# Decoder layer on one core: hand-written steps of a slot replaced by a finer table of ticks

## The reference

```
x = x + attention(layernorm(x))          # 16 heads of 8, causal, rope, keys and values through a latent of 32 with its own norm
x = x + cross_attention(layernorm(x))    # 8 heads of 64, 32 context rows per batch
x = x + ffn(layernorm(x))                # gate/up/down with 352 hidden; inputs and weights rounded to blocks of 16 FP4 values
```

## Time and profile before

| | us |
|---|---|
| median of 3 runs | 427.41 (425.40 to 429.64) |
| the profiled execution: span from first to last instruction | 431.1 |
| busy: PE, DVE, ACT, POOL | 295.3, 301.2, 177.1, 194.2 |

### The profile page before, as it was taken

The page is one execution under the profiler, slowest core; times in us unless marked ns, Lnnn a source line. Parts: engine busy times, 40 slices in busy tenths (PEclk is TensorE's granted clock), DMA queues, the critical chain, the costliest instruction groups (busy, mean ns, idle before and its releaser), DMA issues.

```text
span 431.1 us, 6518 instructions
## 1 busy us (share of the span) xinstructions
PE 295.3 (69%) x1790; PEld 144.0 (33%) x1790; DVE 301.2 (70%) x1137; ACT 177.1 (41%) x327; POOL 194.2 (45%) x374
## 2 busy tenths in 40 slices
PE   1702655777888788787868687787878846657454
PEld 1300233332343222324333334344343314436233
DVE  5426749472666546878886898989978356787872
ACT  5320345563544454443555454454446313222111
POOL 4200216761133534545384745535447353745653
PEclk9999999996766655886997798989969869766696
DMA  6079000043030025002100260030000000000000
GB/s 186 0 207 209 1 0 2 2 149 74 1 75 1 0 76 147 2 2 59 23 8 0 81 149 6 3 79 3 9 6 2 8 0 8 6 1 7 2 13 18
DMA packets 20835, 17.50 MB, mean 41 GB/s; under 512 B 1920, under 2 KB 20224, under 8 KB 20800
## 3 DMA queue, kind: packets, MB, share of 16 engines
q1 hardware_dynamic: 20272, 16.50, 15.7%
q10 hardware_dynamic: 528, 0.59, 0.5%
HBM read 9.62 MB, written 7.34 MB: 39 GB/s over the span
## 4 chain that ended last, share of the span: by engine, by line
PE 36%; DVE 30%; issue 10%; POOL 9%; DMA 7%; ACT 5%; SPq 1%; POOLq 0%; DVEq 0%; ACTq 0%
DVE summed L832 7%; PE pvp L1116 7%; PE st L1105 4%; PE mxp L1081 4%; DMA ks<-parts_dram 3%; PE mxp L1016 3%; DVE space L766 2%; PE misc L1180 2%; DMA parts_dram<-parts 2%; POOL space L473 2%; DVE space L763 2%; PE misc L1195 2%; PE pvp L1127 2%; DVE space L746 2%; ACT probs L633 2%
## 5 line engine op out<-in xcount | busy, mean ns | idle before, releaser
L832 DVE CUSTOM_DVE_ANT_0 summed<-mxp,causal 128x512 bf16<-128x512 f32 (+3 forms) x256 | 114.0, 485 | 28.2 <-PE mxp L1081 27.9
L633 ACT ACTIVATE probs<-st 128x1024 f32<-128x1024 f32 (+1 forms) x96 | 84.6, 881 | 85.4 <-PE st L1105 85.1
L1081 PE MATMUL mxp<-ks,qs 48*128 48x512 bf16 (+3 forms) x256 | 41.4, 362 | 62.2 <-DVE rmax L832 38.6
L443 POOL TENSOR_SCALAR_AFFINE_SELECT probs<-probs 128x256 f32<-128x256 f32 x128 | 49.6, 423 | 24.8 <-ACT probs L633 24.8
L1116 PE MATMUL pvp<-probs,va 128*32 128x128 f32 (+3 forms) x512 | 57.1, 530 | 5.1 <-POOL probs L443 5.1
L543 ACT ACTIVATE space<-misc 128x128 f32<-128x128 f32 (+3 forms) x78 | 24.2, 327 | 50.9 <-PE misc L1136 18.0
L1105 PE MATMUL st<-qs,ks 50*128 50x512 bf16 (+3 forms) x256 | 41.7, 366 | 4.6 <-ACT probs L633 2.5
L1081 PEld LDWEIGHTS mxp<-ks,qs 48*128 48x128 bf16 x256 | 11.9, 98 | 82.6 <-DVE rmax L832 44.6
L473 POOL TENSOR_TENSOR space<-space 128x128 f32<-128x128 f32 (+2 forms) x33 | 24.8, 751 | 19.7 <-DVE space L769 19.7
L434 POOL TENSOR_SCALAR var<-mv 128x1 f32<-128x1 f32 (+1 forms) x36 | 9.1, 253 | 46.1 <-DVE mv L739 44.6
L485 POOL TENSOR_TENSOR space<-space,reciph 128x352 f32<-128x352 f32 x16 | 12.6, 786 | 35.1 <-DVE reciph L757 35.1
(11 more groups left out here) (196 smaller groups left out, 587.9 us busy)
## 6 DMA issues: line engine op xcount, KB each, us to landing
parts_dram<-parts SPq DMA_DIRECT2D x8, 384.0 KB, 2.6
qs<-parts_dram SPq DMA_DIRECT2D x16, 192.0 KB, 3.8
ks<-parts_dram SPq DMA_DIRECT2D x16, 192.0 KB, 4.4
parts_dram<-parts SPq DMA_DIRECT2D x8, 256.0 KB, 2.9
xin<-in_x SPq DMA_DIRECT2D x4, 256.0 KB, 6.2
parts_dram<-parts SPq DMA_DIRECT2D x8, 128.0 KB, 2.9
out<-outr SPq DMA_DIRECT2D x16, 64.0 KB, 1.6
qs<-nrows SPq DMA_DIRECT2D x32, 4.0 KB
```

The source lines that it names most:

```text
L443: last = g.affine_select(out=m, in_=m, compare_op=ALU.is_ge, fill=0.0, base=0, pattern=[[0, 2], [1, P]], channel_multiplier=-1)
L633: nc.scalar.activation(probs[n % 2][:, 2 * pair:2 * pair + 2, 512 * k:512 * k + w], st2[:, :].rearrange("p (h q) -> p h q", h=2)[:, :, 0:w ...
L832: last = v.tensor_tensor_reduce(out=summed[:, m % 2, e * w:(e + 1) * w], in0=mxp[m % 3][:, e * w:(e + 1) * w], in1=causal[:, S - w:S], sca ...
L1081: last = mm(units[r][:, e * w:(e + 1) * w], qs[rows, c, i * P:(i + 1) * P], ks[rows, c, 0:w], start=True, stop=True)
```

## The change

Each piece gets its own moment, a tick, of which a slot has 100. For every kind of piece there is a table of ticks (`SCORE_AT`, `EXP_AT`, `PAIR_AT`, `MAX_AT`, `VALUE_AT`, `ROW_AT` for one row tile's 45 operations, `ROW_AT_END` for tiles 12 to 15, `PROJECT_AT`, `SET_UP_AT`, `WEIGHT_AT`), and each engine walks the ticks from -100 to 2200 and issues what is due. A tick orders the pieces of one engine; no engine waits for a tick. The helpers are split into single operations. Waits, buffers, banks and the operations themselves stay: each engine issues as many instructions as before (the built programs have 1304 on PE, 1139 on DVE, 334 on ACT, 378 on POOL and 125 on SP, both). The part before the first slot stays but for its end: TensorE no longer issues two pairs, nor VectorE three pieces, of slot 1 ahead of the loop; they come in the loop.

```diff
-MAX_STEPS = [((0, 3),), ((0, 4),), ((0, 5), (0, 6)), ((0, 7), (0, 8)), ((0, 9),), ((0, 10), (0, 11)), (), ((1, 0),),
-             ((1, 1),), ((1, 2),)]
-SCORE_STEPS = [0, 1, 3, 5, 6, 8]
-MASK_STEPS = [4, 9]
-SET_UP = [(0, 1), (0, 4), (0, 8), (1, 1), (1, 4), (1, 8), (2, 3), (2, 6), (3, 3), (3, 6), (3, 8)]
+MAX_AT = [-116, -112, -102, -100, -96, -92, -78, -73, -71, -56, -50, -44]
+SCORE_AT = [9, 20, 36, 57, 72, 97]
+EXP_AT = [4, 20, 44, 60, 74, 99]
+MASK_AT = [23, 104]
+ROW_AT = {"attT_mm": 39, "attT": 45, "o_mm": 43, "x1": 47, "stats2": 49, "mv2": 53, "var2": 41, "rstd2": 45, "x1b": 33,
...
+ROW_FIRST = [501, 601, 701, 801, 901, 1001, 1101, 1201, 1300, 1400, 1499, 1600, 1634, 1636, 1648, 1681]
+SET_UP_AT = [-6, 3, 155, 194, 209, 227, 254, 272, 331, 355, 392]
...
-            def round_fp4(norm, expo, norm_name, exp_name, clamp_name, sum_name, n):
+            def exponent(norm, expo, norm_name, exp_name, n):
                 wait(dve, norm_name, n + 1)
                 v.tensor_scalar(expo.bitcast(i32), norm.bitcast(i32), 0x7F800000, None, ALU.bitwise_and)\
                     .then_inc(s[exp_name], 1)
+            def rounding(expo, exp_name, clamp_name, n):
                 wait(dve, exp_name, n + 1)
                 v.tensor_scalar(expo, expo, 1.0, ROUND, ALU.max, ALU.mult).then_inc(s[clamp_name], 1)
+            def add_rounding(norm, expo, clamp_name, sum_name, n):
                 wait(dve, clamp_name, n + 1)
                 v.scalar_tensor_tensor(norm, norm, BIT_DOWN, expo, ALU.mult, ALU.add).then_inc(s[sum_name], 1)
...
-            for n in range(NSLOT + 5):
-                b, g = n // NG, n % NG
-                for u in range(10):
-                    if in_range(n) and u in SCORE_STEPS:
-                        score_unit(n, SCORE_STEPS.index(u))
-                    if u == MAX_ROWS and in_range(n + 1):
-                        max_rows(n + 1)
-                    for stage, k, step in row_work(n, u):
-                        stages[stage](k, step)
...
+            for tick in range(START, END):
+                for n, i in due_slots["score"].get(tick, ()):
+                    score_unit(n, i)
+                for n, _ in due_slots["turn"].get(tick, ()):
+                    if n > 0:
+                        max_rows(n)
+                for k, step in due_rows.get(tick, ()):
+                    row(k, step)
...
```

More of the change, by code:

```diff
@@ L82, in decoder_layer @@
+ROW_FIRST = [501, 601, 701, 801, 901, 1001, 1101, 1201, 1300, 1400, 1499, 1600, 1634, 1636, 1648, 1681]
+SET_UP_AT = [-6, 3, 155, 194, 209, 227, 254, 272, 331, 355, 392]
+WEIGHT_AT = {"max": 28, "scale": 69, "recip": 173, "norm": 177, "exp": 219, "clamp": 251, "sum": 269, "round": 229,
+             "dq": 283}
+START, END = -T, T * (NSLOT + 6)
 def decoder_layer(nc, x, ctx_768, L0_attn_W_q, L0_attn_W_dkv, L0_attn_W_uk, L0_attn_W_uv, L0_attn_W_o,
@@ L298, in decoder_layer, with by_tick @@
         block = ctx.enter_context(nc.Block())
[L307 to L316, removed]
-                if 0 <= at < 40:
-                    work.append(("abcd"[at // 10], k, at % 10))
-            return sorted(work, key=lambda w: ("dcab".index(w[0]), w[1]))
+        def by_tick(steps):
+            due = {}
+            for tick, step in steps:
+                due.setdefault(tick, []).append(step)
+            return due
+        due_slots = {name: by_tick((T * n + at, (n, i)) for n in range(NSLOT) for i, at in enumerate(table))
+                     for name, table in (("pair", PAIR_AT), ("max", MAX_AT), ("parts", PARTS_AT), ("turn", [TURN_AT]),
+                                         ("nrows", [NROWS_AT]), ("place", [PLACE_AT]), ("score", SCORE_AT),
+                                         ("exp", EXP_AT), ("mask", MASK_AT))}
+        due_values = by_tick((T * n + at, (n, i)) for n in range(NSLOT)
+                             for i, at in enumerate(VALUE_AT_END.get(n, VALUE_AT)))
+        due_rows = by_tick((ROW_FIRST[k] + at, (k, step)) for k in range(B * NT)
+                           for step, at in (ROW_AT if k < LAST else ROW_AT_END).items())
+        due_batches = by_tick((T * NG * (b - 1) + at, (b, step)) for b in range(1, B) for step, at in PROJECT_AT.items())
+        due_weights = by_tick((at, step) for step, at in WEIGHT_AT.items())
         @block.sync
@@ L523, in _ @@
             g.memset(vx[:, :, :, :], 0.0).then_inc(s["cross_ready"], 1)
-            stages = {"a": stage_a, "b": stage_b, "c": stage_c}
-            for n in range(NSLOT + 5):
-                b, g_ = n // NG, n % NG
-                for u in range(10):
-                    for stage, k, step in row_work(n, u):
-                        if stage in stages:
-                            stages[stage](k, step)
-                    if b < B - 1:
-                        project(b + 1, g_, u)
-                    if b == 0:
-                        set_up(n, u)
-                    if in_range(n) and u in MASK_STEPS:
-                        mask_probs(n, MASK_STEPS.index(u))
+            for tick in range(START, END):
+                for k, step in due_rows.get(tick, ()):
+                    row(k, step)
+                for b, step in due_batches.get(tick, ()):
+                    project(b, step)
+                for step in due_weights.get(tick, ()):
+                    weights(step)
+                for n, pair in due_slots["mask"].get(tick, ()):
+                    mask_probs(n, pair)
         @block.scalar
@@ L730, in _, with row_stats @@
             v = nc.vector
-            def row_stats(src, stats, mv, name, tiles, n, places=None):
+            def row_stats(src, stats, name, tiles, n, places=None):
                 for t, at in zip(tiles, places or tiles):
@@ L1017, in project @@
                             .then_inc(s["rope_mm"], 1)
+                if step == "values":
+                    values_in(b)
             def values_in(b):
```

517 lines of the change are left out of this document (273 added, 244 removed), and 7 rows, old and new, of tables (PROJECT_AT, WHEN).

## The result

The changed kernel takes **355.5 us** in the median of 4 runs (353.3 to 359.7), the kernel before on the same chip 428.5 (425.4 to 432.9): a ratio of 0.830 (95% interval 0.822 to 0.837). I had predicted 401, in a range of 384 to 429. The direction is right; the gain is 73 us instead of 26, outside the range. The profiled execution spans 355.1 us and answers to the 431.1 of before. In a later group of runs it took 352.3 us. Ratios here leave out executions that were over 1.5% slower than the fastest of their kernel; medians are over all.

The account below looks back on a forecast made before the run. VectorE was taken to set the pace of the late slots, TensorE to lead in slots 0 to 6; +1 - 7 - 14 - 2 - 5 = -27 us gave 404.1 profiled, forecast 401 us, range 384 to 429.

Parts of the forecast that it names:

- Start: Up to the first exponential: two set-up steps now stand ahead of TensorE's first score, +1 us (0 to +2).
- Slots 0 to 6: Spread set-up and scores between longer pieces cut TensorE's idle time: -7 us, bounds a loss of 5 to a gain of 20.
- Rival C: Slots 7 to 14: TensorE's clock stays low and TensorE becomes the bound, +11 us, 438; chance 14%.
- a quarter: Slots 0 to 6: the share of TensorE's 29.9 us idle time taken as saved, giving -7 us.
- Slots 7 to 14: VectorE's single-product waits go and its own time falls: -14 us, bounds zero to -25.
- The link term: Slots 7 to 14: 16 fewer dependent neighbours on VectorE at 0.12 us each, 1.9 us a slot, 15 us in eight.
- the signs that I had named: Slots 7 to 14: length near 140, VectorE's busy time down 10 to 17 us, TensorE's `rmax` wait much shorter than 24.6.
- Slot 15: Until its normalisation: GpSimd's second mask stands behind one division only, TensorE's values behind other row work; -2 us (0 to -5).
- End: After slot 15's normalisation: divisions first and two tiles alternating on VectorE shrink waits and links; -5 us (0 to -10).
- The rounds: At the end: GpSimd's 3.9 us round trip per tile, 1.4 of it waiting for VectorE, expected to disappear.
- Rival A: VectorE operations held by GpSimd's port lock eat the links' 15 us in slots 7 to 14: 413 us; chance 13%.
- Rival B: Whole kernel: the waits only move and new ones eat the links, leaving 427 us (422 to 431); chance 13%.

Follow-up runs that it names:

- the doubled products: The kernel before with each maximum product of slots 5 to 7 issued twice (48 more matmuls): 430.5 us, ratio 1.013.

## Why the prediction was wrong

- **Start**, +1 predicted, +0.6 measured: right.
- **Slots 0 to 6**, -7 predicted, -32.1 measured, beyond even the bound of -20. This is the step that failed most, and the place I had named to look at first. Two errors. I bounded the gain by TensorE's idle time, as if its busy time were fixed; 19.8 of the 32.1 us came out of its busy time, and all but some 2 of those are nearly the same instructions run faster, with the clock of slots 2 to 6 risen. Rival C had the arithmetic of it (3.9 us a slot) but as a side case, and I let slots 5 and 13 speak against a clock that answers to the work; the doubled products lifted it. And I priced the idle time by VectorE's and TensorE's waits, and took "a quarter", without reading ScalarE's wait for scores, 42.6 us in these slots alone and 11.9 after. Idle time on TensorE fell by 12.3 us, where I had taken 7.
- **Slots 7 to 14**, -14 predicted, -22.3 measured, inside its bounds. The link term was right in kind and smaller in size: gluing the chains together again costs 7.2 us of VectorE's time, where I had 15. VectorE's busy time fell only to 125.1 us, not 119. Of the signs that I had named, the wait for `xmax` is gone and TensorE's wait for `rmax` fell from 24.6 to 15.2 us. What I had too low was how full the leading engine could be: 125.1 / 132.4 = 94%, the best slot's share that I had allowed only as a bound.
- **Slot 15**, -2 predicted, -4.8 measured; the bound was -5.
- **End**, -5 predicted, -17.4 measured, beyond the bound of -10. The rounds did go. But VectorE also was busy for 6.7 us less (50.2 to 43.5) and TensorE for 4.9, and the stretch's idle parts on both shrank. The end's new order gained nothing on the old row tiles and some 17 us on the new ones, so it had no price of its own to be put in a sum.
- **Rival A** was real in its mechanism (the norm at 580 ns in the mean instead of 370) and did not matter to the length. I had counted ten operations a row tile as held, where the earlier trace rows show one of them, L755. **Rival B**, waits that only move, is what every partial version built up from before did (433 to 482 us), but for the set-up alone: it was the right fear for a table that does not fit, and I had no way to tell a fitting table from another by its order.
- **Rival C** did not come: in slots 7 to 14 the clock went from 0.87 to 0.91.
- **The sum itself** is the deeper error. I added terms by stretch and by engine as if each edit had its own effect. The runs show that the parts don't add: 8 ticks on one kind of piece are worth 33 or 50 us, and 96 to 99 both together. My reading of it is that each piece must come after its releaser has finished and before its reader stands idle, on both sides at once; the shifts of the scores to either side fit that, and no run shows it for every kind of piece.

What stays open: how much of the 19.8 us of TensorE's time would have come without the shorter waits, and what in the new order raised the clock. The doubled products show that the clock can give back about 5 us in three slots, not how the 32.1 us divide.

## What to carry to other kernels

Where several in-order queues share single-buffered banks, read for every hand-over how long the reader waits and also how long the piece stood behind others after it could have run; the engine with the largest sum need not be the busy one. Such a sum points to a place to look and is not the price: 71.3 us of the same wait went with a run of 370.4 us, 85.1 with one of 428.5. Don't price a reordering as a sum of parts, and don't test it by halves: a table that fits may only show its worth whole, and one that is off by a twelfth of a period can cost more than it gives. Don't take TensorE's busy time as fixed: the same instructions took 254.7 and 262.0 us in two executions of the changed kernel and 313.5 with two of its tables moved by 8 ticks. Put both ends into the range.

## What the runs showed of the hardware

- Redundant matmuls shortened a stretch: 48 more of them, and slots 4 to 6 went from 55.5 to 50.8 us at clocks of 0.81, 1.00 and 0.79 instead of 0.66, 0.58 and 0.67.
- TensorE ran slot 5 of before at a clock of 0.58 with no idle gap over 1.9 us, and slot 5 of the changed kernel at 1.00 with a gap of 2.7 us.
- The clock that the profile prints for the first 80 us is not always that of the products: 1.00 before and 0.50 after in slot 0, with the same pair of products at 2.07 and 2.08 us.
- In the changed kernel nine of 32 norms (128x128, VectorE) began within 0.03 us of GpSimd's 352-wide division of 0.79 us and took 0.88 to 0.89 us instead of 0.34; moving them 8 ticks earlier took the mean of all 32 from 580 to 355 ns.
